# Attention between two frequency-domain layers on one core: queries loaded by half unit, two units' first halves swept first, block 1's chain taken up at once

## The reference

```python
x = L0_attn_x                                   # (4, 1024, 128) float32
x = x + 0.5 * ffn(layernorm(x))
x = x + attn(layernorm(x))
x = x + 0.5 * ffn(layernorm(x))

def ffn(x):    # real(ifft(fft(x) @ w)) + bias, w complex 128x128
def attn(x):
    latent = x @ Wc_down                        # 128 -> 64
    q = (latent @ Wq_up).reshape(B, T, 16, 8)   # 16 heads of 8
    k, v = split(latent @ Wkv_up)               # one k and one v of 8, shared by all heads
    att = softmax(causal(q . k / sqrt(8)))      # T = 1024
    return (att . v).reshape(B, T, 128) @ Wc_proj
```

## Time and profile before

| | |
|---|---|
| median of 3 runs | 618.06 us (616.23 to 618.11) |
| the profiled execution | 615.98 us, of which the span from first to last instruction is 613.9 us |
| first sweep 1 tile | 34.59 us |
| last sweep 1 reduction | before 560 us |
| granted TensorE clock, mean | 0.98 |

### The profile page before, as it was taken

One profiled execution on the slowest core, in us unless ns is written; L12 is line 12 of the kernel. 1 busy time (PEld: TensorE's weight loads), 2 busy tenths in 40 slices (PEclk: granted clock), 3 DMA queues, 4 the chain that ended last, 5 costly groups with the idle time before them and its releaser, 6 DMA issues.

```text
span 613.9 us, 13365 instructions
## 1 busy us (share of the span) xinstructions
PE 583.8 (95%) x5205; PEld 325.9 (53%) x5205; DVE 490.0 (80%) x1258; ACT 380.2 (62%) x834; POOL 89.4 (15%) x311
## 2 busy tenths in 40 slices
PE   7676999999999999999999999999999999999898
PEld 6553664655454555545454546454545555453257
DVE  3762899998889899888899899798888989886023
ACT  2323148366777576776668776857676767677751
POOL 4202111110011312310012312100002110000100
PEclk8878999999999999999999999999999999999899
DMA  6011110011000010011010110011000100000000
GB/s 181 5 42 61 80 47 5 3 44 44 21 24 20 14 55 18 4 34 67 26 40 1 46 40 3 18 32 76 11 31 17 43 3 18 3 4 2 0 18 19
DMA packets 16978, 18.68 MB, mean 30 GB/s; under 512 B 2428, under 2 KB 14556, under 8 KB 16916
## 3 DMA queue, kind: packets, MB, share of 16 engines
q1 hardware_dynamic: 16243, 17.47, 8.4%
q10 hardware_dynamic: 672, 0.36, 0.2%
HBM read 11.90 MB, written 5.24 MB: 28 GB/s over the span
## 4 chain that ended last, share of the span: by engine, by line
PE 82%; ACT 7%; DVE 5%; issue 3%; DMA 1%; POOL 1%; SPq 1%; ACTq 0%; DVEq 0%
PE o_ps L764 22%; PE s1p L714 20%; PE st L738 20%; PE st L742 4%; PE s1p L717 4%; ACT probs L858 4%; PE misc L644 4%; PE st L750 3%; ACT z L840 2%; PE misc L639 1%; DVE mx_pair L1027 1%; DMA wkv<-in_w_kv 1%; PE misc L674 1%; SPq L591 0%; DVE mx L1027 0%
## 5 line engine op out<-in xcount | busy, mean ns | idle before, releaser
L858 ACT ACTIVATE probs<-st 128x512 f32<-128x512 f32 (+2 forms) x640 | 307.3, 564 | 141.1 <-PE st L742 87.3
L1027 DVE TENSOR_REDUCE mx_pair<-s1p 128x1 f32<-128x512 f32 (+3 forms) x432 | 260.2, 660 | 44.1 <-PE s1p L714 33.7
L714 PE MATMUL s1p<-k_sb,q_sb 72*128 72x512 bf16 (+3 forms) x768 | 220.4, 331 | 7.2 <-issue 4.3
L738 PE MATMUL st<-q_sb,k_sb 75*128 75x512 bf16 (+3 forms) x768 | 217.0, 328 | 5.5 <-ACT probs L858 3.6
L764 PE MATMUL o_ps<-probs,v_sb 128*32 128x512 f32 (+3 forms) x1536 | 145.9, 498 | 0.0
L714 PEld LDWEIGHTS s1p<-k_sb,q_sb 72*128 72x128 bf16 x768 | 73.7, 100 | 84.2 <-DVE mx_pair L1027 26.8
L738 PEld LDWEIGHTS st<-q_sb,k_sb 75*128 75x128 bf16 x768 | 73.6, 97 | 81.4 <-ACT probs L858 37.9
L1027 DVE TENSOR_REDUCE mx<-s1p 128x2 f32<-128x256 f32 (+2 forms) x192 | 104.3, 593 | 14.7 <-PE s1p L717 14.0
L717 PE MATMUL s1p<-ident,causal 128*128 128x128 bf16 x512 | 100.8, 222 | 0.0
L742 PE MATMUL st<-causal,ident 128*128 128x128 bf16 x512 | 100.3, 220 | 0.0
L764 PEld LDWEIGHTS o_ps<-probs,v_sb 128*32 128x32 f32 x1536 | 40.4, 110 | 66.9 <-issue 58.4
(11 more groups left out here) (115 smaller groups left out, 342.1 us busy)
## 6 DMA issues: line engine op xcount, KB each, us to landing
q_sb<-q_parts_dram SPq DMA_DIRECT2D x31, 288.0 KB
q_parts_dram<-q_parts SPq DMA_DIRECT2D x24, 128.0 KB
x_sb<-in_x SPq DMA_DIRECT2D x8, 256.0 KB, 4.4
out<-out_sb SPq DMA_DIRECT2D x8, 256.0 KB, 2.3
q_sb<-mT SPq DMA_DIRECT2D x14, 24.0 KB
const<-in_consts SPq DMA_DIRECT2D x1, 320.0 KB, 5.0
q_sb<-q_parts SPq DMA_DIRECT2D x5, 32.0 KB
q_sb<-q_parts ACTq DMA_DIRECT2D x4, 32.0 KB
```

Source lines behind the costliest of these rows:

```text
L714: last = mm(ps[:, e * width:(e + 1) * width], queries[:, h0 + e, at:at + P], k_sb[0:ROWS, b, lo:lo + width], start=True, stop=not diagonal)
L738: last = mm(ps[:, e * w:(e + 1) * w], k_sb[0:ROWS_MAX, b, P * ki:P * ki + P], q_sb[0:ROWS_MAX, slot, c, h0 + e, first:BLK], start=True, st ...
L858: nc.scalar.activation(probs[:, s % PROBS, h0:h0 + per, 0:w], st[n % 3][:, 0:per * w].rearrange("p (e w) -> p e w", e=per), ACT.Exp, scale ...
L1027: v.tensor_reduce(dst, s1p[n % 3][:, 0:heads * width].rearrange("p (e w) -> p e w", e=heads), axis=AX.X, op=ALU.max).then_inc(s1_free, 1)
```

## The change

Queries are loaded half by half. Each half waits only for the store of its own block and, from unit 4 on, for sweep 2 of the chunk that used that half of the slot. Unit 1's first half is loaded as soon as block 0's store has landed; block 1's store is followed by unit 0's second half and then both halves of the rest. Sweep 1 of batch 0 goes through the first halves of units 0 and 1 (12 tiles each), then through their second halves, then on as before. Block 1's `ln2b` and `z2T` move into the written-out start, and its `q`, `kv` and `kT` are taken up 0.7 after the plan's time zero. `LEAD` goes from 12 to 18. The plan's costs of a store and of consecutive loads change. The arithmetic of every tile is the same.

```diff
-LEAD = 12
+LEAD = 18
+LOAD_SPAN = 4.0
...
+def s1_order():
+
+    whole = range(N1)
+    out = [(0, t) for t in range(N1_HALF)] + [(1, t) for t in range(N1_HALF)]
+    out += [(0, t) for t in range(N1_HALF, N1)] + [(1, t) for t in range(N1_HALF, N1)]
+    return out + [(u, t) for u in range(2, UNITS) for t in whole]
...
-LAST_ST = {u: max(n for n, t in enumerate(ST) if GROUP[t[0]][1] == u) + 1 for u in range(UNITS)}
+LAST_ST = {(u, c): max(n for n, t in enumerate(ST) if GROUP[t[0]][1:3] == (u, c)) + 1
+           for u in range(UNITS) for c in range(2)}
...
-LOAD_STEP, STORE_STEP, MAX_STEP = 6.0, 3.0, 2.5
+LOAD_STEP, STORE_STEP, MAX_STEP = 6.0, 5.0, 2.5
...
-    out += [("job", "kT", 0), ("post", "kT", 0)]
+    out += [("job", "kT", 0), ("post", "kT", 0), ("do", "ln2b", 1), ("job", "z2T", 1), ("post", "z2T", 1)]
...
+        self.at(self.pe + STORE_STEP, lambda: self.load(j))
+
+    def load(self, j):
+        if j == 0:
+            halves = [(1, 0)]
+        elif j == 1:
+            halves = [(0, 1), (1, 1), (2, 0), (2, 1), (3, 0), (3, 1)]
         else:
+            halves = [(u, j % 2) for u in range(GROUPS * (j // 2), GROUPS * (j // 2 + 1))]
+        for u, c in halves:
+            self.load_half(u, c)
+
+    def load_half(self, u, c):
+        last = LAST_ST[u - SLOTS, c] if u >= SLOTS else 0
+        if self.n_st < last:
+            self.at(self.pe + .5, lambda: self.load_half(u, c))
+        elif last and self.exp_end[last - 1] > self.pe:
+            self.at(self.exp_end[last - 1], lambda: self.load_half(u, c))
+        else:
+            self.items.append(("sp", "load_q", u, c))
+            self.load_end = max(self.load_end + LOAD_SPAN, self.pe + LOAD_STEP)
+            self.q_at[u, c] = self.load_end
...
-        u, t = divmod(n, N1)
+        u, t = S1_ORDER[n]
...
-        self.chain(PRO_STEPS[5:], 1, self.pro_finished, 3.0)
+        self.at(0.0, lambda: self.load(0))
+        self.chain(PRO_STEPS[7:], 1, self.pro_finished, .7)
...
+            def load_q(u, c):
+
+                sp.wait_ge(q_stored, 16 * PARTS * (2 * (u // GROUPS) + c + 1))
                 if u >= SLOTS:
-                    sp.wait_ge(exp_done, LAST_ST[u - SLOTS])
-                if u:
-                    load_half(u, 0)
-                load_half(u, 1)
+                    sp.wait_ge(exp_done, LAST_ST[u - SLOTS, c])
+                load_half(u, c)
...
-                        pe.wait_ge(q_loaded[slot], 32 * (u // SLOTS) + (32 if slot else 16))
+                        pe.wait_ge(q_loaded[slot][0], 16 * (u // SLOTS) + (16 if slot else 0))
                     pe.wait_ge(k_ready, 2 * b + 1)
                 if t == N1_HALF:
                     pe.wait_ge(k_ready, 2 * b + 2)
-                    if u == 0:
-                        pe.wait_ge(q_loaded[0], 16)
+                    pe.wait_ge(q_loaded[slot][1], 16 * (u // SLOTS + 1))
```

More of the change, by code:

```diff
@@ L62 @@
 N1_HALF = sum(t[0] < NT // 2 for t in S1)
+def s1_order():
[3 more added lines that the diff above has]
+    return out + [(u, t) for u in range(2, UNITS) for t in whole]
+S1_ORDER = s1_order()
 def s2_groups():
@@ L134, in __init__ @@
         self.pv_end = {}
-        self.q_at, self.k_at, self.v_at = {0: [0.0, 1e9]}, {0: 0.0}, {0: 0.0}
+        self.q_at, self.k_at, self.v_at = {(0, 0): 0.0}, {0: 0.0}, {0: 0.0}
         self.max_at = {}
@@ L138, in __init__ @@
         self.sel_done = set()
-        self.stored = 0
-        self.loaded = 1
+        self.load_end = 0.0
         self.pro_next, self.pro_busy = 2, True
@@ L214, in store @@
         self.items.append(("sp", "store_q", j))
[L215 to L231, removed]
-        else:
[L233 to L238, removed]
+        self.at(self.pe + STORE_STEP, lambda: self.load(j))
[4 more added lines that the diff above has]
+            halves = [(0, 1), (1, 1), (2, 0), (2, 1), (3, 0), (3, 1)]
+        else:
+            halves = [(u, j % 2) for u in range(GROUPS * (j // 2), GROUPS * (j // 2 + 1))]
[11 more added lines that the diff above has]
+            self.q_at[u, c] = self.load_end
     def maxima(self, u, part):
@@ L257, in s1_ready @@
             return None
-        if u not in self.q_at or 2 * b + late not in self.k_at:
+        if (u, int(late)) not in self.q_at or 2 * b + late not in self.k_at:
             return None
         free = self.red_end[n - 3] + .1 if n >= 3 else 0.0
-        return max(free, self.q_at[u][late], self.k_at[2 * b + late])
+        return max(free, self.q_at[u, int(late)], self.k_at[2 * b + late])
     def run_s1(self):
         n = self.n_s1
-        u, t = divmod(n, N1)
+        u, t = S1_ORDER[n]
         tb, lo, width, h0, heads, diagonal = S1[t]
@@ L488, in macaron_program @@
         x_loaded = [sem(f"x_loaded{j}") for j in range(BLOCKS)]
-        q_loaded = [sem(f"q_loaded{n}") for n in range(SLOTS)]
+        q_loaded = [[sem(f"q_loaded{n}_{c}") for c in range(2)] for n in range(SLOTS)]
         max_loaded = [sem(f"max_loaded{n}") for n in range(SLOTS)]
@@ L550, in load_half @@
                              src.rearrange("a (d h) t -> (a d) (h t)", h=GH).unsqueeze(0)
-                             .broadcast_to([PARTS, PARTS * HD, GH * BLK])).then_inc(q_loaded[u % SLOTS], 16)
-            def load_q(u):
-                sp.wait_ge(q_stored, 2 * 16 * PARTS * (u // GROUPS + 1))
+                             .broadcast_to([PARTS, PARTS * HD, GH * BLK])).then_inc(q_loaded[u % SLOTS][c], 16)
+            def load_q(u, c):
+                sp.wait_ge(q_stored, 16 * PARTS * (2 * (u // GROUPS) + c + 1))
                 if u >= SLOTS:
-                    sp.wait_ge(exp_done, LAST_ST[u - SLOTS])
-                if u:
-                    load_half(u, 0)
-                load_half(u, 1)
+                    sp.wait_ge(exp_done, LAST_ST[u - SLOTS, c])
+                load_half(u, c)
             def max_rows(u, part, turn):
@@ L600, in _ @@
                 elif item[1] == "load_q":
-                    load_q(item[2])
+                    load_q(item[2], item[3])
                 elif item[1] == "max":
```

## The result

The changed kernel takes 632.49 us (median of 4, 629.83 to 633.12) beside 617.17 for the kernel before (616.23 to 618.11): a ratio of 1.025 [1.023, 1.0271]. It is **slower by 15.3 us**; the forecast was 8.7 us faster. The profiled execution took 629.83, against 615.98 before.

The account below looks back on a forecast made before the run. It took TensorE to bound the kernel from 120 us to sweep 1's end, VectorE from 60 to 80; 3.4 + 2.9 + 3.2 − 0.8 = 8.7 us off 618.06 gave 609.4 us, range 604.8 to 614.6.

Parts of the forecast that it names:

- The loads: Block 1's store lands at 50.0, unit 0's second half at 56.2 instead of 59.26; ring order would make the gain 8.0.
- VectorE in the old hole: Unit 1's first 12 tiles fill VectorE's idle time; unit 0's second half begins at 56.5 instead of 59.88, 3.4 earlier.
- The rival of a wait that moves: Unit 1's first half lands late at 49.5, TensorE waits in order, gain 5.2, time 612.9; chance 0.16.
- The rival that ended slower: SP's in-order waits for sweep 2's slots stop sweep 2 in the three later batches, 625 us; chance 0.06.
- the signs to look for: New profile: store near 42, no VectorE idle above 3 us from 36 to 80, second chunk near 85, hardly any filler after 100.
- half a microsecond at the q product: Block 1's q product, at about 37.0: 0.5 us allowed for a half clock before the store's issue at 42.0.
- The terms 3.4 and 3.2: Sweep 2 of chunk 1 starts 3.4 us earlier; 3.2 us of TensorE filler from 100 to 120 goes.
- The 2.9 for the twelve tiles: At sweep 2's chunk 1 start, sweep 1 is 12 tiles ahead, 0.24 us of TensorE each, 2.9 us saved later.
- The terms at their bad ends: Load at 56.9 plus 1.5 for stalls, filler kept, tail 1.5: some 3.5 us of gain remain.
- The tail's term: After sweep 1's end, six more tiles of lead no longer fill TensorE's gaps: loss of 0.8 us, between 0 and 1.5.

Follow-up runs that it names:

- the kernel with the maxima ahead: Changed kernel with unit 0's first maxima moved ahead of block 1's six load halves on SP's queue: 611.1 us, ratio 0.9899 to the kernel before.
- the best kernel: Changed kernel, unit 0's first maxima ahead of SP's loads, block 2's statistics behind the maxima, 8 filler items, lead 18: 602.88 us, ratio 0.9788.
- the two pairs with 94 filler items: Changed kernel, SP's order kept, 94 filler items in TensorE's wait for the maxima: 629.08 us, ratio 1.0192; executions 632.3 and 632.6, 625.7 and 625.9.

## Why the prediction was wrong

**Up to 50 us it was right, the last figure by luck.** First tile 35.52 (35.8 forecast), q product 37.01 (37.0), store issued 42.72 (42.0), unit 1's first tile 45.81 (45.9) after no wait worth the name, store landed 50.0 (50.0). The store went out 0.7 late and landed on time, 7.3 us after its issue for a forecast 8.0: two small errors cancel.

**The step that failed is in "The loads".** There it says: "On SP only block 1's store and unit 0's maxima stand behind that wait, neither due before 42, so the wait itself costs nothing". That followed what SP waits for at unit 1's first half and stopped there. The next six loads, behind the next wait, were costed only by when they land; that unit 0's maxima go through the same queue, and on which side of these loads, was never asked. In the plan's list the six loads are entries 38 to 43 and the maxima's transfer entry 47, and the plan takes 2.5 us for that transfer (`MAX_STEP`) whatever stands ahead of it. In the kernel before it had gone out at 45.58, ahead of everything, so its landing time had never shown as a wait. The price could have been had from the prediction's own number: six loads of 3.8 us are 22.8; 22.1 was measured.

The rule that the prediction cites from the Trainium skill (DMA: Bandwidth & Descriptors, section "Queues, rings and completion order"), that each engine takes descriptors in ring order, was the right one. The trace agrees with it: 12 KB behind six loads took 20.8 us. The prediction applied it to load and store, where it moved the sum by 0.7 us, and not to these 12 KB.

**A second omission made it dear.** In "VectorE in the old hole" unit 0's second half begins when its queries are there. But sweep 2's first tile of unit 0 stands ahead of it on TensorE, so one late transfer of 12 KB stops both sweeps. The rival of a wait that moves named this very mechanism, TensorE in order behind a late transfer, but with unit 1's first half as the late one, which was in time. The rival that ended slower came nearest: it says that "a unit's maxima may stand behind one" of SP's waits. But it looked for that in the later batches, at the waits for sweep 2's slots; TensorE's waits for maxima are 22.1 us in the whole trace, all in this one of batch 0. Of the signs to look for, one did show it: "no VectorE idle above 3 us between 36 and 80", where 22.27 was measured.

**The clock** stood in the sum with half a microsecond at the q product (0.9 measured there: 2.02 instead of 1.12) and nowhere else. Behind the wait it cost 7 us, and even in the kernel with the maxima ahead some 5. It was in the trace of the kernel before already. The prediction reads 60 to 80 as bound by VectorE, but the first half of 60 to 70 is bound by TensorE at its lower level (window of the kernel before):

```profile
60.00:65.00 5.00, 5.00 (x44) 3.05 (x43) 3.20 (x6) 2.50 (x6) 0.00 (x0) 0.61 0.19 79
```

Of the 2.0 us of VectorE's idle time that the sum takes out of 60 to 80, 1.8 lie here, and filling the wait ahead of it gave the kernel before 0.3% (1.9 us).

**The rest of the sum, without the misplaced transfer.** The terms 3.4 and 3.2 were of the right kind: in the best kernel, with the maxima in time and the clock kept, the second chunk comes 3.9 earlier and all 4.16 of the filler goes. The 2.9 for the twelve tiles were not measured apart. The terms at their bad ends add up to 2.9 us of gain (3.4 − 0.4 − 1.5 + 2.9 − 1.5), not to the 3.5 that the prediction's range starts from. The tail's term had the wrong sign: lead 18 was booked as a loss of 0.8 and measured as a gain of 0.5% alone, 0.6% in the best kernel, and nothing with the maxima ahead. There its profile is at half clock from 60 to 73 at the start, and that of lead 12 from 60 to 70 and for some 3 us of the tail. The prediction had TensorE's gaps in the tail grow with the lead; in the profiles they shrink. Even in the changed kernel some is given back later: sweep 2's second chunk is late by 22.6 us (111.15 for 88.52) and the end by 13.85. How those 8.8 divide among the tiles ahead, the filler and the lead was not measured apart.

## What to carry to other kernels

When transfers are moved, write down the issue order of their queue before and after, and ask of every small one that an engine waits for what now stands ahead of it: here its landing time was the sum of those and not a matter of its size. Then ask what stands behind the waiting instruction on an engine that runs in order, since that is what the wait costs. And count the stretch after a wait at the clock that it will have: here filling the wait with useless products gave back 0.3 to 1.15%.

## What the runs showed of the hardware

- The 12 KB transfer was used 2.3 us after its issue ahead of the loads, landed 20.8 us after it behind six of 288 KB, and 8.5 us after it on another engine's queue beside them. Each load ahead cost 3.6 to 3.7 us of wait.
- The granted clock can stay at half for long behind a short wait: at 0.50 from 60 to 71 us after 3.96 us, with TensorE 10.72 of 11 us busy, and still at 0.50 from 80 to 85 after 1.90 us that followed long filler. The wait of 4.33 before the change cost less: the clock was 0.80 over the next ten microseconds. Near the end of the kernel before it fell with no single gap above 1.21 us, in a stretch (575 to 580) in which TensorE had 2.81 of 5 us of work. Two executions of one program can differ too, as the two pairs with 94 filler items suggest (632 and 626 us). What makes the difference stays open.
